# The last block of a four-block model: weights and x made ready inside the attention before it, maxima spread by a matmul with the identity, eight PSUM banks, casts shared with GpSimd

## The reference

```python
def _act_fake_quant(x, clip_factor):
    scale = jax.nn.sigmoid(clip_factor) * jnp.max(jnp.abs(x)) / QMAX
    return jnp.clip(_ste_round(x / scale), -QMAX - 1.0, QMAX) * scale

def _weight_fake_quant(w):
    scale = jnp.max(jnp.abs(w), axis=1, keepdims=True) / QMAX
    return jnp.clip(_ste_round(w / scale), -QMAX - 1.0, QMAX) * scale
xq = _act_fake_quant(x, clip_x[0])                      # x: layer-normed, (8, 256, 256)
gate = jnp.einsum('bsh,ih->bsi', xq, _weight_fake_quant(w_gate))   # w_gate, w_up: (704, 256)
up = jnp.einsum('bsh,ih->bsi', xq, _weight_fake_quant(w_up))
h = _act_fake_quant(jax.nn.silu(gate) * up, clip_down[0])
return jnp.einsum('bsi,hi->bsh', h, _weight_fake_quant(w_down))
```

## Time and profile before

| what | value |
|---|---|
| median of 3 runs | 998.09 us (996.44 to 1004.11) |
| the profiled execution's own time | 998.65 us |
| its span | 996.9 us |
| TensorE busy | 843.5 us, 85% |
| VectorE busy | 720.1 us, 72% |
| ScalarE busy | 507.2 us, 51% |
| GpSimd busy | 73.2 us, 7% |
| mean granted TensorE clock | 0.92 of full speed |

### The profile page before, as it was taken

The page is one execution under the profiler, slowest core; times in us unless marked ns, Lnnn a source line. Parts: engine busy times, 40 slices in busy tenths (PEclk is TensorE's granted clock), DMA queues, the critical chain, the costliest instruction groups (busy, mean ns, idle before and its releaser), DMA issues. The chain is left out here.

```text
span 996.9 us, 16711 instructions
## 1 busy us (share of the span) xinstructions
PE 843.5 (85%) x5560; PEld 675.4 (68%) x5563; DVE 720.1 (72%) x1646; ACT 507.2 (51%) x1056; POOL 73.2 (7%) x135
## 2 busy tenths in 40 slices
PE   3359999996557659999999989999899999995657
PEld 3247777764334547888888868888688888884223
DVE  6337788774558548888888768788688887775777
ACT  2036666663314125655556546556455565553665
POOL 1000101000130000000000000000000000000241
PEclk9669999999768769999999989999999999998797
DMA  3362222201300040000000000000000000000002
GB/s 103 106 195 81 85 85 85 75 19 30 152 0 1 1 116 12 2 0 12 1 11 2 1 14 2 1 12 1 4 12 1 1 1 1 1 1 18 13 0 85
DMA packets 37518, 33.41 MB, mean 34 GB/s; under 512 B 9586, under 2 KB 36276, under 8 KB 37172
## 3 DMA queue, kind: packets, MB, share of 16 engines
q1 hardware_dynamic: 37428, 32.28, 10.1%
HBM read 17.59 MB, written 2.10 MB: 20 GB/s over the span
## 5 line engine op out<-in xcount | busy, mean ns | idle before, releaser
L1367 ACT ACTIVATE c_probs<-c_pS,c_neg_max 128x512 f32<-128x512 f32 x128 | 88.2, 689 | 120.2 <-DVE c_neg_max L1489 120.1
L1489 DVE TENSOR_REDUCE c_neg_max<-c_pS 128x1 f32<-128x512 f32 x128 | 88.3, 690 | 70.6 <-PE c_pS L1690 68.8
L454 DVE TENSOR_REDUCE a_neg_max<-a_pS 128x2 f32<-128x512 f32 x128 | 82.4, 687 | 17.5 <-PE a_pS L621 17.0
L322 ACT ACTIVATE a_probsT<-a_pT 128x512 f32<-128x512 f32 x128 | 69.6, 597 | 48.3 <-PE a_pT L637 47.3
L1484 DVE TENSOR_TENSOR c_pT_lo<-c_pT,c_pT_hi 128x512 fp32r<-128x512 f32 x128 | 87.1, 681 | 1.3 <-ACT c_pT_hi L1375 1.3
L1707 PE MATMUL c_pO<-c_pT_hi,c_v_hi 128*128 128x256 f32 x256 | 77.4, 302 | 3.1 <-DVE c_pT_lo L1484 3.1
L1697 PE MATMUL c_pT<-ident,c_probs 128*128 128x128 f32 x512 | 77.5, 274 | 0.3 <-DVE c_probs L1496 0.3
L1697 PEld LDWEIGHTS c_pT<-ident,c_probs 128*128 128x128 f32 x512 | 64.3, 142 | 18.2 <-DVE c_probs L1496 0.7
L1380 ACT ACTIVATE c_oT<-c_pO,c_bv 128x256 f32<-128x256 f32 x64 | 30.4, 475 | 85.9 <-PE c_pO L1707 83.2
L1375 ACT CAST c_pT_hi<-c_pT 128x512 fp32r<-128x512 f32 x128 | 74.0, 579 | 0.0
L1707 PE MATMUL c_pO<-c_pT_hi,c_v_lo 128*128 128x256 f32 x256 | 72.0, 281 | 0.0
(11 more groups left out here) (349 smaller groups left out, 2164.6 us busy)
## 6 DMA issues: line engine op xcount, KB each, us to landing
a_k_stack<-a_k_parts SPq DMA_DIRECT2D x96, 64.0 KB, 2.6
a_q_stack<-a_q_parts SPq DMA_DIRECT2D x96, 64.0 KB, 2.6
a_ctx_in<-in_ctx_dram SPq DMA_DIRECT2D x8, 256.0 KB, 2.8
b_raw<-in_L_xattn_Wkv_dram SPq DMA_DIRECT2D x1, 2048.0 KB, 12.2
ctx_in<-in_ctx_dram SPq DMA_DIRECT2D x8, 256.0 KB, 2.7
out_dram<-x_sb SPq DMA_DIRECT2D x8, 256.0 KB, 2.2
x_sb<-in_x_dram SPq DMA_DIRECT2D x1, 1280.0 KB, 6.5
b_raw<-in_L_xattn_Wq_dram SPq DMA_DIRECT2D x1, 1024.0 KB, 7.7
```

The costliest lines, as they stand in the source:

```text
L322: nc.scalar.activation(probsT[:, r // 2 % 2, 2 * (r % 2) + e, :, :], pT[:, e, :, :], ACT.Exp).then_inc(s["exp"], 1)
L454: nc.vector.tensor_reduce(neg_max[:, r // 2 % 2, :, e, r % 2], pS[:, e, :, :], AX_X, ALU.max, negate=True).then_inc(s["max"], 1)
L1367: nc.scalar.activation(probs[:, u % 4, :], pS[:, u % 2, :], ACT.Exp, bias=neg_max[:, u % 4:u % 4 + 1], accum_out=sums[:, u % 4:u % 4 + 1]) ...
L1489: nc.vector.tensor_reduce(neg_max[:, u % 4:u % 4 + 1], pS[:, u % 2, :], AX_X, ALU.max, negate=True).then_inc(s["max"], 1)
```

## The change

Nothing changes in what is computed apart from the order of scalings (the scale of up is applied to the row maxima and to h's quantizer, not to each product). The parts:

1. **attention1** takes over work of ffn1. GpSimd makes `ident_b` and `ones_row`, after batch 0's scaling the bf16 of the gate and up weights (`wb`), and in batch 7 that of w_down (`db`). VectorE makes w_down's scales and int8 in batch 7 at u = 0 and 2. TensorE transposes the weights in batch 7 (`turn_w`, after u = 9, 11, 13, 15, six bf16 transposes each), ScalarE copies them out (`wt_out`, at u = 10, 12, 14 and after the loop).
2. **x by features.** `out_normed` writes into `c_ob`; TensorE turns the batch in float32 (`turn_x3`, four transposes into `c_pQ`, at u = 13 of the next batch), ScalarE copies it to `xT3` at u = 14 (`x3_out`). For batch 7 both come after everything else. ffn1 no longer transposes x: it scales `xT3` to int8 and casts it.
3. **Clips**: loaded and passed through the sigmoid in `slots0`.
4. **Maxima over partitions**: `ones_row` times the maximum, a float32 matmul with the identity, and a VectorE reduction of the PSUM row, in place of both `partition_all_reduce`.
5. **Gate and up**: three banks each in place of two, four `silu` buffers as before; one VectorE reduction for two tiles; ScalarE's copy of up without a scale; x's chunk 0 split between ScalarE and VectorE, chunks 1 to 3 on GpSimd (int8, then bf16).
6. **Down**: the cast to bf16 is VectorE's for even tiles and GpSimd's for odd ones; eight banks, one for each batch of the output, so no matmul waits for `scaled`; GpSimd adds batches 0, 2, 4, 6.
7. `c_probs` has two buffers in place of four, and `exps` waits for the transposes of the unit before the last (the instruction ahead of it on ScalarE already waits for those).

The core of the diff:

```diff
@@ slots0, SP and ScalarE
+            sp.dma_start(clips[:, 0:1], a["L1_ffn_clip_x"].partition_broadcast(P)).then_inc(s["load_c"], DMA)
+            sp.dma_start(clips[:, 1:2], a["L1_ffn_clip_down"].partition_broadcast(P)).then_inc(s["load_c"], DMA)
+            act.wait_ge(s["load_c"], 2 * DMA)
+            nc.scalar.activation(clips[:, :], clips[:, :], ACT.Sigmoid).then_inc(s["clip"], 1)
@@ attention1, GpSimd
             kv_norms(1)
+            pool.wait_ge(s["w8"], 4)
+            for k in range(2):
+                nc.gpsimd.tensor_copy(wb[:, k, 0:FT - 1, :], ffn_w8[k][:, 0:FT - 1, :])
+                nc.gpsimd.tensor_copy(wb[0:FR, k, FT - 1, :], ffn_w8[k][0:FR, FT - 1, :]).then_inc(s["wb"], 1)
...
+            power(rstd_o, var_eps_o, "var_o", "rstd_o", B - 2)
+            pool.wait_ge(s["d8"], 1)
+            for c in range(DC):
+                nc.gpsimd.tensor_copy(db[c], d8[:, c, :]).then_inc(s["db"], 1)
+            power(rstd_o, var_eps_o, "var_o", "rstd_o", B - 1)
@@ attention1, ScalarE, in batch
+                    if last and u in (10, 12, 14):
+                        wt_out(u // 2 - 5)
+                    if u == 14 and not first:
+                        x3_out(b - 1)
                     if u % 2 == 0:
                         if not first or u > 0:
                             out_turned(g - 1, (u // 2 - 1) % H1)
...
             by_twos(act, batch)
+            wt_out(3)
             out_turned(H1 * B - 1, H1 - 1)
+            x3_out(B - 1)
@@ attention1, VectorE
+                if last and u == 0:
+                    down_scales()
+                if last and u == 2:
+                    down_whole()
@@ attention1, TensorE, in batch
                         values(b, u // 2)
+                        if last and u >= 9:
+                            turn_w(u // 2 - 4, (s["k_lo"], H1 * B - 1) if u == 9 else (s["k_lo"], H1 * B) if u == 11 else (s["wt_sb"], u // 2 - 4))
+                        if u == 13 and not first:
+                            turn_x3(b - 1)
...
             out_project(B - 1, H1 - 1)
+            pe.wait_ge(s["x3_sb"], B - 1)
+            turn_x3(B - 1)
@@ ffn1
+        by_pool = lambda n: n % 2 == 1 and n < NTILE - 1
+        pG = pb("e_pG", [P, 3, CH])
+        pU = pb("e_pU", [P, 3, CH])
+        pY = pb("e_pY", [P, 2, CH])
+            def x_parts(k):
+                pool.wait_ge(s["xinv"], 1)
+                pool.wait_ge(s["hzero"], 1)
+                if k >= 2:
+                    pool.wait_ge(s["up"], FT * (k - 1))
+                nc.gpsimd.tensor_scalar(x8[:, k % 2, :, :], xT3[:, :, CH * k:CH * (k + 1)], xscale[:, 1:2], None, ALU.mult).then_inc(s["x8"], 1)
+                pool.wait_ge(s["x8"], k)
+                nc.gpsimd.tensor_copy(xT[:, k % 2, :, :], x8[:, k % 2, :, :]).then_inc(s["xT"], 1)
-            nc.gpsimd.partition_all_reduce(xmax[:, 1:2], xmax[:, 0:1], P, bass.bass_isa.ReduceOp.max).then_inc(s["xall"], 1)
+            nc.vector.tensor_scalar(spread[:, 0, :], ones_row[:, :], xmax[:, 0:1], None, ALU.mult).then_inc(s["xspread"], 1)
+            nc.tensor.matmul(pG[:, 0, 0:P], spread[:, 0, :], ident[:, :], start=True, stop=True).then_inc(s["xrow"], 1)
+            nc.vector.tensor_reduce(xmax[:, 1:2], pG[:, 0, 0:P], AX_X, ALU.max).then_inc(s["xall"], 1)
+            nc.scalar.mul(x8[:, 0, 0, :], xT3[:, 0, 0:CH], xscale[:, 1:2]).then_inc(s["x8_act"], 1)
+            nc.vector.tensor_scalar(x8[:, 0, 1, :], xT3[:, 1, 0:CH], xscale[:, 1:2], None, ALU.mult).then_inc(s["x8_dve"], 1)
+            nc.vector.tensor_copy(xT[:, 0, :, :], x8[:, 0, :, :]).then_inc(s["xT_first"], 1)
+                nc.vector.tensor_reduce(hmax[:, i:i + 2, k], h[:, i:i + 2, CH * k:CH * (k + 1)], AX_X, ALU.max, apply_absolute_value=True).then_inc(s["hmax"], 1)
+                nc.gpsimd.tensor_copy(hb[0:r, k % 2, i, :], h8[0:r, k % 2, i, :]).then_inc(s["hb_pool"], 1)
-                if b >= 2:
-                    pe.wait_ge(s["scaled"], b - 1)
```

More of the change, by code:

```diff
@@ L1729, in batch @@
                         v_before = (s["k_lo"], g + 2) if last and u == 10 else (s["v_lo"], g + 4)
+                        if last and u == 10:
+                            pe.wait_ge(s["wt_sb"], 1)
                         if u < 12:
@@ L1821, in ffn1, with bank_of @@
         scaled = sb("e_scaled", [P, 2, TT, D])
[L1823 to L1830 removed]
+        pG = pb("e_pG", [P, 3, CH])
+        pU = pb("e_pU", [P, 3, CH])
+        pY = pb("e_pY", [P, 2, CH])
+        pW = pY[:, :, :].bitcast(BF16)
+        def bank_of(b):
+            return pG[:, b, :] if b < 3 else pU[:, b - 3, :] if b < 6 else pY[:, b - 6, :]
+        names = """zero hzero dT dT_sb dcol drow xmax xspread xrow xall xs xinv gus x8_act x8_dve x8 xT_first xT gate up silu up_sb
+                   h_dve h_pool hmax hm hmax1 hspread hrow hall hs hinv hscale fscale h8 hb_dve hb_pool y scaled res
+                   res_pool out""".split()
         s = {k: sem("e_" + k) for k in names}
[L1834 to L1835 removed]
         DOWN_TURNS = []
@@ new lines, in _, with to_bf16 @@
+            for n in range(NTILE):
+                if by_pool(n):
+                    product(n)
+                if n in (FT + 3, 2 * FT + 3):
+                    x_parts(n // FT + 1)
+            def to_bf16(n):
+                k, i = divmod(n, FT)
+                r = rows_of(i)
+                pool.wait_ge(s["h8"], n + 1)
+                if k >= 2:
+                    pool.wait_ge(s["y"], 2 * (k - 1))
+                nc.gpsimd.tensor_copy(hb[0:r, k % 2, i, :], h8[0:r, k % 2, i, :]).then_inc(s["hb_pool"], 1)
@@ new lines, in residual @@
+            def residual(b):
+                pool.wait_ge(s["scaled"], b + 1)
+                nc.gpsimd.tensor_tensor(x_sb[:, TT * b:TT * (b + 1), :], scaled[:, b % 2, :, :].rearrange("p t d -> p t d"), x_sb[:, TT * b:TT * (b + 1), :], ALU.add).then_inc(s["res_pool"], 1)
+            for n in range(1, FT, 2):
+                to_bf16(n)
+            for k in range(NCH):
+                if k + 1 < NCH:
+                    for i in range(1, FT, 2):
+                        to_bf16(FT * (k + 1) + i)
+                residual(2 * k)
@@ L1889, in _ @@
[L1889 to L1910 removed]
+            act.wait_ge(s["xinv"], 1)
@@ new lines, in size @@
+            def size(n):
+                k, i = divmod(n, FT)
+                dve.wait_ge(s["h_dve"], done_dve(n + 2))
+                dve.wait_ge(s["h_pool"], done_pool(n + 2))
+                nc.vector.tensor_reduce(hmax[:, i:i + 2, k], h[:, i:i + 2, CH * k:CH * (k + 1)], AX_X, ALU.max, apply_absolute_value=True).then_inc(s["hmax"], 1)
+            dve.wait_ge(s["hzero"], 1)
+            for n in range(NTILE):
+                if not by_pool(n):
+                    product(n)
+                if n % 2 == 0 and n >= 2:
+                    size(n - 2)
```

389 lines of the change are left out of this document (178 added, 211 removed).

## The result

The changed kernel takes 1002.82 us (median; 1000.08 to 1006.0), the kernel before, run beside it, 999.67 us. The ratio is 1.0034 with a 95% interval of 1.0019 to 1.005: no faster, 0.3% slower, where 983.7 us was predicted. The profiled span went from 996.9 to 1001.1 us. TensorE is busy 852.5 us of it (843.5 before), GpSimd 98.8 (73.2).

What follows compares the result with a forecast made beforehand. It took TensorE to bound the attention, and VectorE and waits at two global maxima the last block. 7.0 - 8.6 - 6.4 - 3.7 - 2.7 = -14.4 gave span 982.5 and median 983.7 us, range 976 to 992.

Steps and rivals of the forecast that it cites:

- Gate and up: Last block, first silu to last reduction: 31.3 us before, 24.9 forecast, -6.4 (23 to 30 us for it).
- nearer to the casts: Gate and up: why GpSimd's single-input passes over 1024 elements were priced at 1.3 us, between 1.05 and 2.5.
- 19.2 together, 24 at the high price: Gate and up: GpSimd's summed work in us, 11 products (14) plus four passes over 1024 elements.
- first rival: GpSimd bounds the last block: gate and up +3, preparation +1.5, down +6.4, total 994.6 us; chance 0.13 for 988 to 996.
- sign of being wrong: Gate and up: the forecast is wrong if, among other signs, GpSimd's passes over 1024 elements take over 2 us.
- rival at 1005.7: TensorE gets no full clock in the last block: gate and up 18 us more, down 4 more; chance 0.03.
- Attention: Second attention, with added transposes, copies and casts: +7.0 us, at least 3, at most 11.
- 4.25 counted for batch 7: Attention's last batch: us lost to weight and x transposes and to copies ahead of or behind the last outputs.
- 2.2 for batches 1 to 6: Attention: us lost to four float32 transposes of x in each of six batches, 0.36 each time on TensorE.
- Preparation: Last block's start to first silu: 14.7 us becomes 6.1, -8.6 (5.5 to 9 us for it).
- Scale of h: Last block, last gate-and-up reduction to ScalarE's first quantization: 6.0 us becomes 2.3, -3.7 (3.2 to 4.2).
- Down: Last block, first quantization to end of span: 26.8 us becomes 24.1, -2.7; lowest 21.8, highest 30.5.

Runs made afterwards that it cites:

- Run 1: Changed kernel with GpSimd's int8 and bf16 passes of x's chunks 2 and 3 placed two products earlier; 997.28 us, ratio 0.9987 to the kernel before.
- run 2: Kernel of Run 1 with the int8 pass of x's chunks 2 and 3 moved from GpSimd to ScalarE; 990.65 us, ratio 0.9924.
- run 10: Changed kernel with one of four float32 transposes of x per batch left, copies whole, so a wrong x; 999.56 us, ratio 1.0005.
- run 11: Kernel before with two buffers of probabilities instead of four, exponential's wait adapted; 1001.13 us, ratio 1.0014.
- run 9: Changed kernel with each group's six weight transposes cut to one and its copy from 704 to 128 columns; 999.64 us, ratio 1.0017.
- run 4: Changed kernel with GpSimd's memset of h's empty rows held until VectorE has made the first column; 1000.53 us, ratio 1.0008.
- Run 6: Changed kernel with both maxima over partitions back on GpSimd's all-reduce; 1016.64 us, ratio 1.0153.
- run 8: Kernel of run 7 with 20 unread matmuls keeping TensorE busy through the scale of h; 988.81 us, ratio 0.9876.
- run 12: Kernel of run 7 with GpSimd's three casts of h's last chunk moved to ScalarE; 987.5 us, ratio 0.9889.
- run 7: Changed kernel with the edits of Run 1, run 2 and run 4, plus batch 7's copies behind what TensorE waits for; 988.12 us, ratio 0.9874.

## Why the prediction was wrong

**Gate and up** is the step that failed: forecast 24.9 us, measured 37.8, against a sum of -14.4 in all. Two things in it were wrong. The pass of 1024 float32 elements to int8 on GpSimd was put at 1.3 us "nearer to the casts", with 2.5 as the high end; it takes 2.84, 3.14 beside VectorE, above both. The cast of 1024 int8 elements was put at the same 1.3 and takes 1.04: the rows of casts priced the cast and not the pass. Second, and worth more, the passes were only summed up ("19.2 together, 24 at the high price"). At the measured prices GpSimd's sum is 11 x 1.27 + 2 x (2.84 + 1.04) = 21.7 us, still inside the 24.9. What counts is where the passes stand: behind the products of tile n = 9 and n = 15, so that the first starts at 947.35, 0.26 us after TensorE has finished the chunk (946.10 + 1.27 there is the product ahead of it). The whole 3.9 us are exposed, and the clock, which the prediction had at full speed from the fourth microsecond on, adds 1.5 to 1.7 us at each of the two. Run 1 shortens the waits by place alone, with every instruction unchanged, run 2 takes them to 0.40 and 0.33 us by place and by engine, and 4.7 and 11.0 us come back by the ratios. The "+3" that the first rival gave gate and up at the high price came from the same sum and was as blind to the place. The prediction's own sign of being wrong, GpSimd's passes over 2 us, did come; the price that it had tied to it (994.6 in all) was too low. Its rival at 1005.7 lies nearest to the measured time by luck: TensorE had its full clock in gate and up except at the start and behind the two waits.

**Attention**, +7.0 forecast, +9.8 measured. Between the marks on GpSimd: 0.3 before 486, 4.3 from there to the last mark but one (before: 486.10 to 891.77; after: 486.38 to 896.36), 4.1 in the last stretch (23.01 to 27.11) and 1.1 behind it. The 4.25 counted for batch 7 was 5.2. The 2.2 for batches 1 to 6 was 4.3: three periods grew by 0.48, the last one (831.32 to 896.36, it ends in batch 7) by 1.2, and two, over which the loop turns and which differ by up to a microsecond between kernels alike there, by 1.7 together. Three transposes less gave 0.34 in run 10, so four cost 0.45, a quarter more than the 0.36 read in the earlier trace rows; the buffers cost nothing (run 11). The 0.7 us more of the last period lie where batch 7 has VectorE's scales of w_down, which the prediction put at nothing. VectorE in the changed kernel there:

```profile
856.65 0.69 DVE L1525 TENSOR_REDUCE c_neg_max<-c_pS 128x1 f32<-128x512 f32 x1 [1.13 <-PE c_pS L1771]
...
857.86 1.61 DVE L1559 TENSOR_REDUCE c_dmax<-wd_raw 128x2 f32<-128x1408 f32 x1
...
861.41 0.68 DVE L1525 TENSOR_REDUCE c_neg_max<-c_pS 128x1 f32<-128x512 f32 x1
```

From one row maximum to the next it is 4.76 us, where the kernel before has 856.87 - 852.77 = 4.10 at the same place; no run takes the scales out. In the last stretch 1.5 us stay in run 9 (24.51 for 23.01). They are not the transposes of x, whose loss left the stretch as it was (run 10). Still in it are a sixth of the weights' transposes with short copies, the copy of x ahead of `out_turned` and GpSimd's casts of w_down; which of them it is was not taken apart.

**Preparation**, -8.6 forecast, -7.2 measured. The steps were right, but one was missing: the memset of h's empty rows held the first step of the chain for 1.5 us (run 4: 6.0 us without it, 6.1 forecast). The prediction had the lock among its rows and applied it to casts and products alone. The Trainium skill (SBUF — State Buffer, section "Who interferes with whom") says that the loser of the lock waits for the whole instruction; the trace agrees, with 1.81 us for 0.28.

**Scale of h**: 2.3 forecast, 2.7 measured. Run 6 shows that the edits on the two maxima are together worth about 12 us in this kernel, since an all-reduce also holds up what follows it on GpSimd: with it the scale of h itself is only 1.3 us longer, and down 5.7.

**Down**: 24.1 forecast, 25.2 measured. The clock came back 10 to 12 us after ScalarE's start, sooner than the 14 assumed, and the stage was longer than forecast all the same; in its first 4 us the clock does not matter (run 8). GpSimd's casts took 0.61, less than the 0.8, in the first two chunks. What was missing is at the end: both engines' last three casts take 2.3 and 2.6 us beside each other and follow an addition; with ScalarE in GpSimd's place the stage is 0.9 us shorter (run 12). The first rival's bound in down, +6.4, did not come.

**The sum**: -14.4 forecast. The five misses are +2.8, +1.4, +12.9, +0.4 and +1.1, 18.6 together, which takes -14.4 to the measured +4.2 of the span. Without the 10.0 us that run 2 gets back in gate and up the forecast would have been 8.6 us too low instead of 18.6, and run 7, with the edges, the memset and the copies mended, came within 5 us of it (988.12 for 983.7).

## What to carry to other kernels

A sum of busy times bounds a pipelined stage from below only; for each result that a later stage needs at a fixed point (the next chunk's operand), put down where it stands in its engine's queue and when the consumer will ask for it, and price the slower clock after the wait as well as the wait. An engine that seems to have room in the sum should be given work whose result nobody waits for next. Price a conversion from float32 apart from one from int8: rows of the one say nothing of the other on GpSimd.
